# A decoder layer with a recurrence, cross attention and a butterfly feed-forward on one core: the high butterfly stages as matrix products, and an earlier preparation of the first feed-forward pair

## The reference, cut to what matters

```python
# x (4, 2048, 512), ctx (4, 77, 512)
x = x + attn(layernorm(x))      # linear recurrence along axis 0 (4 steps), independent for all else
x = x + xattn(layernorm(x), ctx, Wq, Wk, Wv, Wo)      # 16 heads, 77 keys
x = x + ffn(layernorm(x), ...)

def ffn(x):
    h = x @ W_exp + b_exp                  # 512 -> 2048
    h = butterfly(h, up_weights, 2048)     # 11 stages, stride 2**stage
    h = gelu(h + up_bias)
    h = butterfly(h, down_weights, 2048)
    return h @ W_con + b_con + down_bias   # 2048 -> 512

def butterfly(y, weights, dim):
    for stage in range(11):                # pairs of features that lie 2**stage apart
        na = w00 * a + w01 * b
        nb = w10 * a + w11 * b
```

## Time and profile before

| | |
|---|---|
| runs | 2370.11, 2364.82, 2364.71 us; median 2364.82 |
| profiled execution | 2366.6 us, span 2364.8 us, clock 0.971 |
| PE busy | 2226.1 us, 94% of the span |
| DVE busy | 1769.8 us, 75% |
| ACT busy | 1293.1 us, 55% |
| POOL busy | 557.2 us, 24% |
| chain that ended last | PE 65%, DVE 16%, ACT 11%, issue 4%, DMA 3%, POOL 1% |

### The profile page before, as it was taken

One profiled execution on the slowest core, in us unless ns is written; L12 is line 12 of the kernel. 1 busy time (PEld: TensorE's weight loads), 2 busy tenths in 40 slices (PEclk: granted clock), 3 DMA queues, 4 the chain that ended last, 5 costly groups with the idle time before them and its releaser, 6 DMA issues.

```text
span 2364.8 us, 42243 instructions
## 1 busy us (share of the span) xinstructions
PE 2226.1 (94%) x15752; PEld 1943.3 (82%) x15752; DVE 1769.8 (75%) x2969; ACT 1293.1 (55%) x2832; POOL 557.2 (24%) x619
## 2 busy tenths in 40 slices
PE   8877789999999999969999999999999999999998
PEld 4777668778777877748998998988989989989898
DVE  5999668878878887755875867857858758678567
ACT  2998556666667666543644635535536446355343
POOL 3788222222222322200030030020210300300203
PEclk9888879999999999989999999999999999999999
DMA  8555702332332232256568677676685686776765
GB/s 329 192 178 189 263 2 77 116 124 77 108 116 94 85 119 90 95 182 219 172 219 267 199 218 227 208 262 179 212 263 177 214 266 200 223 221 210 225 188 177
DMA packets 190883, 424.47 MB, mean 179 GB/s; under 512 B 27342, under 2 KB 64718, under 8 KB 190286
## 3 DMA queue, kind: packets, MB, share of 16 engines
q1 hardware_dynamic: 190696, 421.94, 55.1%
HBM read 331.29 MB, written 90.60 MB: 178 GB/s over the span
## 4 chain that ended last, share of the span: by engine, by line
PE 65%; DVE 16%; ACT 11%; issue 4%; DMA 3%; POOL 1%; SPq 0%; DVEq 0%; ACTq 0%; POOLq 0%
PE ps L416 52%; PE ps L1805 5%; ACT es L982 5%; PE ps L1773 2%; DVE gl L1178 2%; DVE G L1530 2%; DVE st L1149 2%; DVE ptl L1178 1%; DVE wc_s L1178 1%; PE ps L1784 1%; DMA xa<-in_x 1%; DVE rsum L1401 1%; ACT wc_h L939 1%; DVE rmax L1390 1%; ACT pth L957 1%
## 5 line engine op out<-in xcount | busy, mean ns | idle before, releaser
L416 PE MATMUL ps<-ring,gh 128*128 128x256 f32 x3584 | 654.4, 285 | 12.6 <-DVE gl L1178 12.5
L416 PEld LDWEIGHTS ps<-ring,gh 128*128 128x128 f32 x3584 | 558.0, 192 | 16.9 <-DVE gl L1178 15.7
L416 PE MATMUL ps<-xth,ring 128*128 128x512 f32 x1792 | 554.6, 390 | 4.2 <-ACT U L1066 4.2
L416 PE MATMUL ps<-ring,gl 128*128 128x256 f32 x1792 | 506.8, 283 | 0.0
L416 PEld LDWEIGHTS ps<-xth,ring 128*128 128x128 f32 x1792 | 337.4, 188 | 74.7 <-issue 4.6
L1054 ACT ACTIVATE gh<-G 128x512 fp32r<-128x512 f32 x384 | 237.2, 629 | 212.4 <-PE ps L416 212.1
L416 PE MATMUL ps<-xtl,ring 128*128 128x512 f32 x896 | 349.5, 390 | 0.0
L416 PEld LDWEIGHTS ps<-ring,gl 128*128 128x128 f32 x1792 | 343.4, 192 | 0.0
L1178 DVE TENSOR_TENSOR gl<-G,gh 128x512 fp32r<-128x512 f32 x384 | 278.8, 739 | 57.2 <-ACT gh L1054 55.6
L759 POOL TENSOR_TENSOR es<-es,rinv 128x308 f32<-128x308 f32 x256 | 180.2, 735 | 456.5 <-DVE rinv L1405 456.5
L1470 DVE TENSOR_TENSOR U<-ps,U 128x512 f32<-128x512 f32 (+1 forms) x168 | 137.3, 817 | 169.5 <-PE ps L416 166.9
(11 more groups left out here) (212 smaller groups left out, 4646.0 us busy)
## 6 DMA issues: line engine op xcount, KB each, us to landing
ring<-wup_scratch SPq DMA_DIRECT2D x224, 512.0 KB, 3.8
ring<-wdn_scratch SPq DMA_DIRECT2D x224, 512.0 KB, 3.6
X<-x_scratch SPq DMA_DIRECT2D x32, 1024.0 KB, 8.5
xa<-in_x SPq DMA_DIRECT2D x16, 1024.0 KB, 5.5
x_scratch<-xa SPq DMA_DIRECT2D x16, 1024.0 KB, 4.3
x<-x_scratch SPq DMA_DIRECT2D x16, 1024.0 KB, 5.6
x_scratch<-x SPq DMA_DIRECT2D x16, 1024.0 KB, 4.3
out_x<-X SPq DMA_DIRECT2D x16, 1024.0 KB, 6.3
```

Of the source, the lines that this page charges most:

```text
L416: mm = pe.matmul(bank, a, b, start=first and i == 0, stop=last and i == n - 1, skip_group_check=go_on)
```

## The change

1. **High stages as matrix products.** The vector work on xu and yd in the recurrence is gone (xu_back, bup_back, up_mul, up_add, dn_*). Instead each position in a chunk gets its 16x16 matrix over chunks (paths), made on VectorE in the preamble (`bit_masks`, `pick_bit`, `join`) from weights that a broadcast DMA lays out over 128 partitions (hw, 1 MB for each side instead of 64 KB). GpSimd spreads it to a block matrix mq with `high_matrix` (two products of 2048 elements). Features are regrouped between low and high stages by DMA.
2. **66 pieces.** LU: 16 low up products; BL: the bias through the low stages; UH: 16 high up ones, each four 128x128 products that come out turned; BH: the bias through the high stages; DH: 16 high down ones; DL: 16 low down ones. All use fp32, two banks (6, 7) in turn; ScalarE copies each into one of 8 stage tiles, SP sends it on. They stand in the groups of the recurrence as PER_GROUP says. So the chunk products of the preamble and the folds behind the recurrence are gone from their places.
3. **Recurrence.** Unrolled; the products' results go to two banks (4, 5) instead of four; xa has 5 slots; VectorE's adds alternate with low parts. Transposes and queries of attention group 0 stand in the last group.
4. **Tail.** stats3, apply3 and the rsqrts of the first pair move from turn NG to turn NG-1, its transposes to the head of turn NG, its splits earlier in turn NG. The seven first ring loads are issued before the last weights' store instead of after it.

```diff
+        PER_GROUP = [6, 6, 5, 0, 4, 4, 4, 5, 4, 4, 4, 4, 0, 5, 5, 6]
+        def pieces_at(g, c):
+            first, m = group_end(g) - PER_GROUP[g], PER_GROUP[g]
+            return range(first + (m * c + 3) // KC, first + (m * c + m + 3) // KC)
...
+            by_row = lambda w: w.rearrange("q s k e -> q (s k e)").unsqueeze(0).broadcast_to([MC, P, HIS * (MC // 2) * 4])
+            sp.dma_start(hw[0][:, :, :, :, :, :], by_row(hi_up)).then_inc(hw_loaded[0], 16)
+            sp.dma_start(hw[1][:, :, :, :, :, :], by_row(hi_dn)).then_inc(hw_loaded[1], 16)
...
+            sp.dma_start(ubg[:, :], upbias.rearrange("(l j) c -> c l j", j=MC), allow_slow_non_contiguous=True).then_inc(bias_loaded, 16)
...
             store_x2(NG)
-            store_wc(NG - 1)
-            sp.wait_ge(wc_stored, 32 * NG)
             sp.wait_ge(pe_slot, SLOTS * NG + V_SLOT[-1] + 1)
             for n in range(RING):
                 load_ring(n)
+            store_wc(NG - 1)
+            sp.wait_ge(wc_stored, 32 * NG)
...
+            low_paths(wgd, False, lo_loaded[1], tdn_ready)
             rsqrt(1, xn1_ready, T)
+            for g in range(NG - 1):
+                rsqrt(g + 2, xn1_ready, T * (g + 2))
+                if g < 2:
+                    high_matrix(g)
...
+            for g in range(NG):                                    # ScalarE
+                for c in range(KC):
+                    for d in {0: (0, 1), 1: (2, 3)}.get(c, ()):
+                        if g + 1 < NG:
+                            hi1_piece(g + 1, d)
+                    if c > 1 and g + 2 < NG:
+                        apply1(g + 2, range(2 * c - 4, 2 * c - 2))
...
+                    for n in pieces_at(g, c):
+                        piece_back(n)
...
                 residual(3, -2)                                    # VectorE
+                if g == NG - 1:
+                    stats3(0)
                 if g == NG:
-                    stats3(1)
...
+                    split_first(0, 2)
+                    mix_x(0, 1)
                 shift(1)
                 lo_v(0)
...
+            def out1(g, c):                                        # TensorE
+                n = KC * g + c
+                after(pe, x1_ready, max(n - 1, 0))
+                pe.wait_ge(lo1_done, n + 1)
...
+            def piece(n):
+                after(pe, piece_act, max(n - 1, 0))
+                bank = ps[:, 6 + n % 2, :]
...
+                    for k in range(KC):
+                        cols = slice(k * P, (k + 1) * P)
+                        mm = pe.matmul(bank[:, cols], xg[:, j, cols], mq[0][:, j, :], start=True, stop=True)
...
+            for g in range(NG):
+                if g + 1 < NG:
+                    t1(g + 1)
...
+                for c in range(KC):
+                    for n in pieces_at(g, c):
+                        piece(n)
+                    out1(g, c)
...
+                if g == NG:
+                    pe.wait_ge(e_ready, T * NG)
+                    pe.wait_ge(exp_ps, T * NG)
+                    for i in range(4):
+                        turn3(0, i, i)
                 turn_p(2, -1)
                 project(2, -2)
```

More of the change, by code:

```diff
@@ L571, in load_wc @@
             def load_wc(n):
-                for j in range(4):
-                    sp.wait_ge(fold_stored[j], 16 * 2)
+                for out in stage_out:
+                    sp.wait_ge(out, stage_turns(PIECES))
                 after(sp, wc_stored, 32 * n)
@@ new lines, in pick, with pick_bit @@
+            def pick(out, first, second, b):
+                picks(V.tensor_scalar(out, first, bits[:, b, 0:1], None, ALU.mult))
+                return V.scalar_tensor_tensor(out, second, bits[:, b, 1:2], out, ALU.mult, ALU.add)
+            def pick_bit(m, i):
+                b = HIS - 1 - i if m == 0 else i
+                cur, left = rest[m][i], HIS - i
+                if i == 0:
+                    dve.wait_ge(bits_step, 1)
+                    dve.wait_ge(hw_loaded[m], 16)
+                if m == 0:
+                    ends = cur[:, :, b].rearrange("p j q o i -> p j (q o) i")
+                    last = pick(sel[m][b][:, :, :, :].rearrange("p j q o -> p j (q o)"), ends[:, :, :, 0], ends[:, :, :, 1], b)
+                else:
+                    for o in range(2):
+                        last = pick(sel[m][b][:, :, :, o], cur[:, :, b, :, 0, o], cur[:, :, b, :, 1, o], b)
+                if left > 1:
+                    to = rest[m][i + 1][:, :, :, :, :, :]
+                    if m == 0:
+                        part = cur[:, :, :, :, :, :].rearrange("p j s (h q) o i -> p (j s) h (q o i)", h=2)
+                        to = to.rearrange("p j s q o i -> p (j s) (q o i)")
+                    else:
+                        part = cur[:, :, :, :, :, :].rearrange("p j s (q h) o i -> p (j s q) h (o i)", h=2)
+                        to = to.rearrange("p j s q o i -> p (j s q) (o i)")
+                    last = pick(to, part[:, :, 0], part[:, :, 1], b)
+                picks(last)
@@ new lines, in join @@
+            def join(m):
+                n = 2
+                at = range(HIS) if m == 0 else range(HIS - 1, -1, -1)
+                first = sel[m][at[0]][:, :, 0, :]
+                outs = [tree[m][0][:, :, :], tree[m][1][:, :, :], paths[m][:, :, :]]
+                for s, out in zip(at[1:], outs):
+                    w = sel[m][s]
+                    if m == 0:
+                        new = out.rearrange("p j (o l) -> p j o l", o=2)
+                        old = first.unsqueeze(2).broadcast_to([P, MC, 2, n])
+                        w = w[:, :, :, :].rearrange("p j l o -> p j o l")
+                    else:
+                        new = out.rearrange("p j (h i) -> p j h i", i=2)
+                        old = first.unsqueeze(3).broadcast_to([P, MC, n, 2])
+                        w = w[:, :, :, :]
+                    ins = V.tensor_tensor(new, old, w, ALU.mult)
+                    if 2 * n < MC:
+                        picks(ins)
+                    first, n = out, 2 * n
+                ins.then_inc(path_ready, 1)
@@ L1733, in turn3 @@
+            for o in range(2, KC):
+                query(ps[:, o, :], o).then_inc(pre_pe, 1)
+            pe.wait_ge(x1_ready, KC * NG)
+            pe.wait_ge(piece_act, PIECES)
             def turn3(p, i, bank):
```

693 lines of the change are left out of this document (319 added, 374 removed).

## The result

The changed kernel takes 2443.26 us (median of 4 runs, 2439.66 to 2444.9), the kernel before 2364.77 beside it: ratio 1.032, 95% interval 1.0304 to 1.0337. I had forecast 2363.4 and a range up to 2386. The profiled execution's span is 2440.1 us, against 2364.8: 75.3 us to find.

What follows compares the result with a forecast made beforehand. VectorE was taken to bound the recurrence, with TensorE the bound after. A recurrence gain of 5.7 us less a tail loss of 4.3 made 1.4 us faster, 2363.4 us by the median, range 2343 to 2386.

Steps and rivals of the forecast that it cites:

- What bounds it: Recurrence: VectorE, busy 179.6 of 181.2 us before, stops being the bound and TensorE becomes it.
- TensorE's sum: Recurrence: 197.8 us of work, plus 3.4 latency and 7.4 clock, is 208.6 to the last query, 1.4 more until scores.
- the price of a small product with new weights: High up pieces: 0.149 us a record, so 1.15 a piece, 18.4 in all; lower bound 0.89 from a transpose's 0.111.
- charged 7.4: Recurrence clock: 2.2 us for each of two bias pieces and 3 for the start out of an idle stretch.
- A turn with four pieces: Recurrence: ScalarE's normalization ends 1 us before it is wanted, each copy two pieces ahead, no other wait.
- The start: Second group's transposes, opening the recurrence: 65.6 us instead of 62.0, range 62.7 to 70, with wgd landing at 52.9.
- is queued behind the six down-path products: Preamble: GpSimd's rsqrt follows 9.17 us of products waiting for wgd; paths end at 62.1, rsqrt 63.4.
- the new picks ... hide here: Preamble: VectorE's picks, about 9 us up and 9 down, are covered; uncovered they would cost about 5 us.
- TensorE doesn't hold its clock: Recurrence rival: at a stretch of 1.11 the 197.8 us become 219.6, +14.4, 2378 us; chance 0.30.
- The tail: Attention to feed-forward: values at 1035.1, store lands 16.0 us after them, third up product at 1067.0; 4.3 us lost.
- would gain 5: Tail: were the store not delayed by the moved ring loads, it would land 9 to 10 us earlier.
- The slow case: Clock rival at a stretch of 1.15 with a start at 70 us: 2388 us.

Runs made afterwards that it cites:

- e10: e5 with xg and yd loaded in four parts each, yg over groups 3 to 6, bias store ahead of the loads, ring loads behind the last weights' store: 2394.1 us.
- e5: Changed kernel with both regroupings through DRAM, down pieces stored already in new order so the 4 MB yd load is plain: 2401.75 us, ratio 1.0153.
- e12: Changed kernel with low-up pieces going to xg partitions c, c+16, ... instead of eight neighbours, yg load plain, bias load in eight transfers: 2420.2 us, ratio 1.023.
- e9: e5 without GpSimd's six path products on wgu (a single column is written), those on wgd kept: 2398.2 us, ratio 1.0127.
- e8: Kernel before with part 4 (Tail) alone, but the seven ring loads put back behind the last weights' store: 2366.3 us, ratio 1.0003.
- e6: e5 with all picks of the down matrix moved ahead of K's low parts on VectorE: 2408.8 us.

## Why the prediction was wrong, point by point

- *What bounds it, and TensorE's sum: right in the total, in part by luck.* 10.8 us for a group with four pieces, 9.1 without (123.23 to 132.36 in e10), 12.4 with six (88.98 to 101.36 after), 207 us in all (e10) against my 210 once waits are taken off. But the price of a small product with new weights was mis-sized. I read 4.76 us for 32 one-column records as full clock, and it was not: the granted clock was 0.74 there. In e5 the same 32 records ran at 1.00, in 3.68 us. The windows of the kernel before and of e5:

```profile
56.94:61.70 4.76, 4.76 (x33) 4.67 (x31) 1.96 (x5) 2.93 (x4) 2.21 (x3) 0.74 1.03 377
```
```profile
110.45:114.13 3.68, 3.68 (x35) 3.68 (x35) 0.69 (x1) 0.89 (x2) 0.00 (x0) 1.00 0.90 323
```

  That is 0.115 us a record instead of 0.149. The 107 ns that the prediction quotes from the Trainium skill ("TensorE: Matmul & The Clock Gate", section "LDWEIGHTS (loading the stationary operand)") and set aside is the nearer of the two. The high up pieces show it: I took 1.15 us each, and a group of 10.79 less 1.78 and 5.5 leaves 0.88 a piece, the lower bound, the transposes' row. That is 4.3 us too much, and about 2.2 more for the 66 bias records. The clock was mis-sized the other way: without these excesses the 197.8 us of products are about 191, and e10's TensorE was busy 204.9 at 0.92, so by this estimate the clock cost some 14 us where I had charged 7.4. The earlier trace rows also have TensorE busy 29.7 of the first 41.4 us; that it "waits for its first weights" is true of only a part of them.
- *The step that failed: what else the pieces issue.* "A turn with four pieces, followed engine by engine with these durations, shows no other wait": engine by engine, but not transfer by transfer. The 64 pieces' stores and regroupings, 16 MB, had no price in my sum, not even a line that names them. 32 of them are regroupings, and the 16 of xg run at 57 GB/s. In the changed kernel that shows as TensorE's waits of 22.2 and 12.5 us, and as late x. e12 gives back 24.7 us by the partitions, e5 38.3 (274.4 to 236.1) by taking both regroupings through DRAM. The rest down to 210 (26 us in e5, 18 in e10) is of the size of the waits that are left (18.05 and 10.4 us in e5, 9.4 and 7.8 in e10). That the same TensorE work would run free of them is inferred from those brackets; no run removed them all.
- *The start: 65.6 forecast, 74.9 measured.* The step that failed is the path: the rsqrt "is queued behind the six down-path products". It was not, even before. GpSimd stood idle between those products and the rsqrt, waiting for VectorE's statistics, 5.7 us in the kernel before and 7.5 after. Its timelines before and after:

```profile
57.32 1.01 POOL L694 TENSOR_TENSOR rstd<-var_e,mhalf 128x4 f32<-128x4 f32 x1 [5.71 <-DVE var_e L1167]
```
```profile
71.97 1.01 POOL L704 TENSOR_TENSOR rstd<-var_e,mhalf 128x4 f32<-128x4 f32 x1 [7.46 <-DVE var_e L1158]
```

  So "the new picks ... hide here" failed too. For the up matrix they took 7.7 us (16.32 to 23.99; some 9 estimated) and did hide. For the down matrix the first three operations took 8.4 us beside GpSimd instead of 1.1, and the V products, the first transposes and the statistics queue behind them. e9 puts 6.5 us on that. In e9 the rsqrt follows GpSimd's products by only 0.66 us, so there the forecast path binds: what is left, 68.5 against 65.6, is wgd's landing, 55.7 instead of 52.9.
- *The clock: my rival "TensorE doesn't hold its clock" had the sign and about the size, but it isn't the main loss.* The granted clock was below 0.93 from 112 to 300 in the changed kernel (0.68 to 0.86), and TensorE stood waiting there. In e10 it was 0.93 and 0.97 up to 236, and 0.88 behind, where its two long waits are. The whole stretch from the second transposes to the first scores, with the same number of records, in the changed kernel and in e10:

```profile
74.92:349.34 274.42, 213.47 (x1362) 185.38 (x1363) 132.74 (x305) 122.50 (x202) 31.93 (x43) 0.85 0.74 194
```
```profile
79.78:307.99 228.21, 204.86 (x1362) 176.30 (x1363) 131.99 (x305) 122.46 (x202) 32.03 (x43) 0.92 0.78 271
```

  The busy time differs by 8.6 us, the idle time by 37.6. Against the forecast, which had 205.2 us of work and clock and 4.8 of waits in this stretch, the changed kernel is busy 8.3 us longer (some 15, if the over-priced records are taken out; the rival's price was 14.4) and idle 56.2 longer. The low clock went with the idle time; no run sets the clock by itself.
- *The tail: right in mechanism, a loss 2.4 us too small.* ScalarE's wait for the store was forecast at 10 us or more and was 15.4; the store lands 17 us after the values (16.0 forecast); values 12.0 us later counted from the first scores (10.5 forecast); loss 6.7 (4.3 forecast). That without the moved loads part 2 "would gain 5" was wrong: e8 shows zero.
- *The range* left out the one case that came: no rival priced a transfer that isn't in the trace of before. The nearest row of before was be, 10.2 us for 8 KB in the earlier trace rows, which I used for the tail and not here. The slow case, given as 2388, adds up to 2390 from its own terms (22.3 and 4.4 on top of 2363.4).

## What to carry to other kernels

When work moves from vector engines to TensorE as matrix products with a change of layout between them, price the layout's transfers first: how many partitions each writes, how many engines its outer dimension feeds, and what of the next loads queues behind it. Let the DRAM side carry the permutation and keep the SBUF side at 128 rows; a regrouping of 256 KB into eight neighbouring partitions held the queue for about 4.6 us. Small VectorE operations on SBUF, like these picks, aren't hidden when GpSimd has a long product on SBUF beside them. And a row is at full clock only when the granted clock of its own window says so.

## What the runs showed of the hardware

- Transfers of 256 KB into eight neighbouring partitions: 57 GB/s; into eight spread by 16: 107; 4 MB in 8 x 16 blocks of 32 KB: 94 over its 44.5 us; 4 MB as 128 rows: 318 over its 13.2 us. The first two hold a DMA share of 0.54, the last one's window 0.95.
- VectorE operations on SBUF of 0.3 us took up to 4.6 us beside GpSimd's products, and ended with them (39.02 and 38.89 in the changed kernel, 40.13 and 40.10 in e6). Not every one was: V's low part, which reads PSUM, took 0.68 us at 60.52, in the middle of wgd's products (55.07 to 64.5), and in e9 four statistics that read x from SBUF took no longer than elsewhere beside wgd's products (55.71 to 64.86), VectorE's timeline:

```profile
56.07 2.46 DVE L1156 BATCH_NORM_STATS2 st<-xa 128x6 f32<-128x512 f32 x4
```

  By the Trainium skill, "SBUF — State Buffer", section "SBUF: two separate sides", the two engines share one pair of ports by an exclusive lock held for the whole instruction, which VectorE needs for an operation in a two-port mode or with two SBUF inputs beside a GpSimd operation that reads SBUF. The trace agrees: the path products with two SBUF inputs were held (2.29 us instead of 0.43), the statistics with one weren't. That the picks ran in a two-port mode is not shown.
- The 32 records of the one-column bias products took 3.68 us at a granted clock of 1.00 (e5), 4.76 at 0.74 (before) and 6.99 at 0.50, the lower of the two levels (in the changed kernel, at 116.79 behind a wait of 4.7 us).
